# A chain of four cross-attention layers: the value projections of the small attentions as whole 128x128 tiles, placed by head parity on ScalarE

## The reference, cut to what matters

```python
# layer 1
V = (a @ Wv.T).reshape(B, Ta, HEADS, HEAD_DIM).transpose(0, 2, 1, 3)
# layer 2, for ctx (x there) and for x (latents there)
kv = (h @ kv_w + kv_b).reshape(b, p + k_len, NH, DH, 2)
# layer 3, self and cross
qkv = ln_out @ w_qkv + b_qkv
kv = encoder_states @ w_kv + b_kv
...
return jnp.einsum('bhqk,bhkd->bhqd', probs, v)
```

## Time and profile before

| what | before |
|---|---|
| median of 3 runs | 1386.85 us (1385.67 to 1387.0) |
| the profiled execution | 1382.49 us, its span 1380.5 us |
| PE busy | 1287.4 us, 93% |
| PE's weight loads | 975.6 us, 71% |
| VectorE, ScalarE, GpSimd busy | 76%, 59%, 56% |
| L671 (values), records | 1280 in five groups of 256 |
| L882 (placing the values), instructions | 160 |

### The profile page before, as it was taken

One profiled execution on the slowest core, in us unless ns is written; L12 is line 12 of the kernel. 1 busy time (PEld: TensorE's weight loads), 2 busy tenths in 40 slices (PEclk: granted clock), 3 DMA queues, 4 the chain that ended last, 5 costly groups with the idle time before them and its releaser, 6 DMA issues. The chain is left out here.

```text
span 1380.5 us, 34075 instructions
## 1 busy us (share of the span) xinstructions
PE 1287.4 (93%) x12668; PEld 975.6 (71%) x12668; DVE 1049.5 (76%) x2226; ACT 808.0 (59%) x2101; POOL 770.8 (56%) x1056
## 2 busy tenths in 40 slices
PE   6999999999999989999899999999999999979675
PEld 5767668686877868677686867768676776857464
DVE  4788896868789696977968787796969878685642
ACT  4657575565657565565666657565655746554332
POOL 2564575556657474665665557565655656563431
PEclk9999999999999999999999999999999999999896
DMA  8100000000000000000000000000000000000000
GB/s 315 37 3 17 2 19 9 17 11 5 18 6 17 11 17 11 6 17 7 17 7 22 6 10 17 8 17 11 16 11 2 21 7 2 7 1 6 1 4 5
DMA packets 23584, 25.72 MB, mean 19 GB/s; under 512 B 10624, under 2 KB 22912, under 8 KB 23168
## 3 DMA queue, kind: packets, MB, share of 16 engines
q1 hardware_dynamic: 23424, 23.55, 5.4%
HBM read 21.44 MB, written 2.10 MB: 17 GB/s over the span
## 5 line engine op out<-in xcount | busy, mean ns | idle before, releaser
L588 POOL TENSOR_SCALAR p_a<-p_a,rec_a 128x256 f32<-128x256 f32 x512 | 245.8, 497 | 99.1 <-DVE rec_a L543 98.8
L574 ACT ACTIVATE p_a<-bank,nmax_a 128x256 f32<-128x256 f32 x512 | 236.8, 476 | 91.3 <-DVE nmax_a L536 90.7
L536 DVE TENSOR_REDUCE nmax_a<-bank 128x2 f32<-128x512 f32 x256 | 166.9, 680 | 13.5 <-PE bank L486 13.2
L601 PE MATMUL bank<-ident,p_a 128*128 128x128 f32 x1024 | 144.7, 277 | 6.0 <-POOL p_a L588 2.7
L486 PE MATMUL bank<-k_a,q_a 64*128 64x256 f32 x1024 | 138.7, 396 | 2.9 <-ACT p_a L574 1.1
L617 PE MATMUL attended<-p_a,v_a 128*64 128x256 f32 x1024 | 133.9, 389 | 4.2 <-DVE p_a L635 1.6
L601 PEld LDWEIGHTS bank<-ident,p_a 128*128 128x128 f32 x1024 | 113.7, 141 | 33.6 <-issue 25.2
L486 PEld LDWEIGHTS bank<-k_a,q_a 64*128 64x128 f32 x1024 | 91.7, 186 | 32.9 <-issue 22.6
L574 ACT ACTIVATION_READ_ACCUMULATOR p_a<-bank,nmax_a 128x1 f32 x512 | 105.8, 207 | 0.0
L617 PEld LDWEIGHTS attended<-p_a,v_a 128*64 128x64 f32 x1024 | 65.4, 136 | 54.5 <-issue 27.9
L635 DVE COPY p_a<-bank 128x512 f32<-128x512 f32 x128 | 86.1, 679 | 14.7 <-PE bank L601 14.3
(11 more groups left out here) (235 smaller groups left out, 3098.7 us busy)
## 6 DMA issues: line engine op xcount, KB each, us to landing
wb<-in_wb SPq DMA_DIRECT2D x1, 4096.0 KB, 12.6
wc<-in_wc SPq DMA_DIRECT2D x1, 4096.0 KB, 24.3
xc<-in_x SPq DMA_DIRECT2D x16, 128.0 KB, 2.7
xc<-in_ctx SPq DMA_DIRECT2D x16, 128.0 KB, 2.9
c_top<-in_ctx SPq DMA_DIRECT2D x16, 128.0 KB, 2.8
res_a<-in_x SPq DMA_DIRECT2D x16, 128.0 KB, 2.1
k_c<-in_ctx SPq DMA_DIRECT2D x16, 128.0 KB, 2.1
out<-y_out SPq DMA_DIRECT2D x16, 128.0 KB, 1.7
```

Of the source, the lines that this page charges most:

```text
L536: dve.tensor_reduce(nmax_a[:, n, e, :], ps[:, :].rearrange("p (q k) -> p q k", q=KT), AX.X, ALU.max, negate=True).then_inc(A.s["max"], 1)
L574: last = act.activation(p_a[:, j % 2, n, e, qt, :], ps[:, qt * D:(qt + 1) * D], ACT.Exp, bias=nmax_a[:, n, e, qt:qt + 1], accum_out=sum_a[ ...
L588: last = pool.tensor_scalar(p_a[:, j % 2, n, e, qt, :], p_a[:, j % 2, n, e, qt, :], rec_a[:, n, e, qt:qt + 1], 1.0, ALU.mult, ALU.mult)
L601: last = nc.tensor.transpose(ps[:, kt * D + qt * P:kt * D + (qt + 1) * P], p_a[:, j % 2, n, e, qt, kt * P:(kt + 1) * P], ident[:, :])
```

## The change

`pe_values` makes two matmuls instead of eight: all 128 tokens of the pair are the stationary operand, and all 256 columns of the weights are the moving one. The output has the sequence in its row half and the heads in their order. `act_values` makes four copies instead of two, one for each sequence b and parity e, from the bank's row half b to the row half e of `T.v`; where b and e differ, input rows and output rows are different ones. Semaphores and fills are the same in kind and number. The strings of `ORDER` for all five engines, and `BANK`, are written anew: the same letters, each as often as before, in another order. The first letters of SP's and PE's stand here.

```diff
     "sp": (
-        "nssdbenkfdbekfbekfdnkbdnbednkeyfbdnkeyf...
+        "nksskfednbkfedfbebdnkbdnbednkeyfbdnkeyf...
     "pe": (
-        "nnsnnaaaaaaddaadddddaadddsskddkddaaknsddkddnddddkdkakaaadknnkbddakbabakadd...
+        "nknsnnaakaaaaddaadddddaadddsdddnaaddkdsddnkddksdaddaaakdannkbddbabakkkddak...
...
         def pe_values(T, i, name, w, srcT):
             ps = fill_bank(T, nc.tensor, i, name)
-            wv = w.rearrange("p k (g e d) -> p k g e d", e=2, d=HD)
-            for b in range(2):
-                for k in range(KT):
-                    for e in range(2):
-                        last = mm(ps[e * S:(e + 1) * S, b * P:(b + 1) * P], srcT[:, k, b * S:(b + 1) * S], wv[:, k, :, e, :],
-                                  start=k == 0, stop=k == KT - 1)
+            for k in range(KT):
+                last = mm(ps[:, 0:D], srcT[:, k, :], w[:, k, :], start=k == 0, stop=k == KT - 1)
             filled(T, last, i, name)
...
             ps = wait_fill(V, act, i, name)
-            for e in range(2):
-                last = act.activation(T.v[e * S:(e + 1) * S, c, :, :, e, :],
-                                      ps[e * S:(e + 1) * S, 0:D].rearrange("p (b g d) -> p b g d", b=2, d=HD), ACT.Copy)
+            for b in range(2):
+                heads = ps[b * S:(b + 1) * S, 0:D].rearrange("p (g e d) -> p g e d", e=2, d=HD)
+                for e in range(2):
+                    last = act.activation(T.v[e * S:(e + 1) * S, c, b, :, e, :], heads[:, :, e, :], ACT.Copy)
             release(V, last, i, name)
```

More of the change, by code:

```diff
@@ L99 @@
[L99 to L103, removed]
@@ new lines @@
+        "bcbkeakeeeecddeacddcddcddaaaddfnnfabeedadbefddeaaeddedandfdfafdkdnefkkeefdeekkkffbfcfkcckcbdbaadbddcbaaeddeeee"
+        "cddecddcaacdadfafeedbdfaneddebaneddedffnaafekdfeedfdkekeffkkkfbnfkddcdakccbbcabcdbddeaeeeeddedccdaddcaadcdanae"
+        "edbdfbnfddfaeendeddeaadaddffddfneafkeedfdeedfkkfkkkkkbcfcdaccfbbacabdddbdddeaeeeedeccdcannacbdbeedaaefedfdndfa"
+        "deddeddaadffdnfaaefkekefkddeekkkkkbfddcfcccbfbcbabfeaeedeececdcddcddadadanfbfbeefnaeeddeaddendadffdafedkfekefk"
+        "aeekffknbfckccfckkdcdbddbdaabddbcdcedeeeeaecdcddddaadaadfnfbebfdaneeedaeddefdfdafnddekfaneefdkkaekfkbkeffkckbd"
@@ L137 @@
-        "aaaekedeaaffaafaaaeeafkkbbbbfbbeeckckdbbccffdccccaecaecaadadeeeeaecefefeddfffdffffkeeeeffefeeccffkbbkbbkbbfcfc"
-        "ccbcceecceeeeeeecefffeeffeffeffeeccccffcfcccfccfffcfffffffffffffff"),
-    "pool": (
[L140 to L146, removed]
+        "nnknssnknnaaaaaaaaaaadsaadaaaaaddfaanbeasnaaadaaadskanndksadaaaaadanaankkdnakabbaabadbbaabkaandnaadanakaabbaaa"
@@ new lines @@
+        "eaaaefdaaaadnnaffanffffdakeeaaeaandaffefeaaeecacffkfnfbbnccbbdbbkcccdccbbaaceaaeadeeaeeeeaacdfdafeadeaafakkaaf"
+        "fdaaffnfafdnaeaekneaaanadaafafefaenndkffeeccbbbbkffbkcbkcccdcbbcaaeceaadaceeaeeeeaacdfadafeaaaefdaanffnffaffdk"
+        "deaeaaaeaaaaffaafaeaefkkbbbbfbbeecdckkbbccffdccccaecaecdaaadeeaeeecefefeddfffdffffekeeeffefeeccffkbbbkbkbfbccf"
+        "ccbcceecceeeeeeeecfffeeffeffeffeeccccfffccccfccfffcfffffffffffffff"),
+    "pool": (
+        "ssnkaaaaaaaaaaaaaakanakkkaaaakkkaababkaknaaaaeeaaaeekkaeaaeaabbaaaeaeaacecnaaccaaaacceeccaaeffaeaaakffkaakffna"
+        "aeaaffaakaakkkbbcccceecceeccffeaaaeffakkkaffaaaenaaffaakkccbbaakkcceaeccaceecffeaaefafakkfkfaaeaanffaaaacckkbb"
+        "cckaceceakceecaaffeaaeaakfkfakafafaeaanfafacckkkkbbccaacceaeaceecffeaaeaaffakkkfafaaeaaffaacckkkknbbccaacceeee"
+        "accafeafaeaaaakffkkfaafeanafaafaacckkkkbbccaaccceeceeaaefefaaaakffaakkffeanaaaffaaaacckkkkbbcccceecceeffeaaeff"
+        "aakkkffaaeaaffaacakkcankkccbbccccaaeeaeeaffeaaeaffakkkffaaeaaffnaakkaakkccbbcccceecceeaaaaffeaaeaakfkfkaaffnaa"
+        "eaaffaakkccccbbkkcccaeeacaeeaffeaaeaaaffkkkaffeaaaffaccaakknccbbckckceecaeeaaaffeeaaaaffkkkfafaeaaaaffaankkcck"
+        "kbbcccceeceeacaaaffeaeaaffakkkffeaaaaffaaaakkkkbbcceeccccceceaaaaffeekffkkffeffcckkkkbbcccceeeecceeffkefkfffcc"
@@ L167, in fill_places @@
+    "426301452613546124063512346150324615032461503246150324610532461360561302564130254321054321025524653240165324601624"
+    "160260534261452034562103642510642530462153046215340650602165304261530215024653102104160431256041325602650264513062"
+    "140351642035164203516403516403516240351460324605321460532165403216540321654032165043216504215603421560342156034215"
+    "60342156034215603421560342156034125603412")
 def fill_places():
```

87 lines of the change are left out of this document (40 added, 47 removed).

## The result

The changed kernel takes 1378.58 us (median; 1378.4 to 1379.38) against 1386.64 us. The ratio is 0.9944, with a 95% interval of 0.9927 to 0.9961; a second, longer measurement beside another set of runs gave 0.9950 (0.9935 to 0.9964). So the change saves 7 to 8 us, 0.5 to 0.6%. The forecast had the sign right and the size wrong: 17.0 us.

A forecast was written before the change was run, and what follows sets the result against it. It took PE's queue to bound some 1200 of 1380 us: 22.0 - 1.5 - 0.4 - 1.7 - 0.8 - 0.65 = 17.0 us less, so 1386.85 - 17.0 = 1370 us. The range was 1360 to 1381 us.

The forecast's parts named there:

- The price of a change of shape: On PE, each array-shape change between neighbouring steps costs 0.15 to 0.20 us; 133 fewer at 0.165 us save 22.0 us.
- The rival that the price belongs to each change of line or bank: On PE, only the number of steps counts, which stays 1492: 1387 us, no change; chance 0.05.
- part 2: PE's new order: 32 fewer shape changes, 5.3 us; price bounded at 0.14 to 0.20 us each.
- Streaming: In PE's value projections, the streaming itself doesn't shrink: 0.88 us of the old step against 0.87 us after.
- ScalarE: Value copies: four of 269 ns replace two of 376 ns, 26 us more on ScalarE, 0.8 us of it reaching PE.
- The start: On SP, an extra load issued ahead of the raw weights delays PE's first weight product: +0.65 us.
- What of it counts: How much of PE's 22.0 us reaches the run: 1.5, 0.4 and 1.7 us off for last tenth, first tenth and middle.
- The term for growing waits: In PE's middle stretch, a tenth is taken off as waits on other engines become relatively later: -1.7 us.
- the tail: Last tenth of PE's order, a chain over other engines: half of 3.0 us (18 changes) counts, -1.5 us.
- a middle share of PE below 95%: Sign against the forecast: PE's busy share in the middle falling below 95%, where the same 97% was expected.
- waits in the place of work: Rival: over half the saving becomes PE's waits on VectorE, ScalarE and GpSimd softmax chains; 1378 us, chance 0.17.

The follow-up runs named there:

- e3: Kernel before, with each value projection copied by ScalarE in four instructions of 64x128 instead of two of 64x256, none changing rows: ratio 1.0017 to before.
- e4: Changed kernel with the two 64x256 value copies of before put back in place of four of 64x128: ratio 0.9946 to before.
- e1: Changed projection and copies, with the queue orders and banks of the kernel before: ratio 0.9972 to before.
- e5: Changed kernel with one of the two matmuls of each value projection left out: median 1377.26 us, ratio 0.9920 to before.
- e7: Changed kernel with VectorE's row maxima of the big attention taken over half of each row's columns: median 1362.13 us, ratio 0.9817 to before.
- e9: Kernel before with VectorE's row maxima of the big attention taken over half of each row's columns: ratio 0.9900 to before.
- e13: Changed kernel with VectorE's big-attention row maxima over half the columns and GpSimd scaling only half the probability columns: ratio 0.9762 to before.

## Why the prediction was right or wrong

**The price of a change of shape: right.** 0.10 us on leaving and 0.05 to 0.10 on entering carried over to the new steps: L668 at 0.87 us, its neighbours at 1.78 and 1.73 us. Over the run there are 133 changes fewer, 21.9 us by this price; no single row measures that sum, and the page's busy time of PE fell by 16.3 us. The trace agrees here with the Trainium skill's rule that a change of tiling mode drains TensorE ("TensorEngine Tiling (Array Packing)", Key Properties). The rival that the price belongs to each change of line or bank falls: eight records of L662 with the same shape on both sides take 0.89 us (median of 18 rows before), and the next row is always another line or bank. One bound in part 2 is wrong: at the paces that it states, the records from 50 to 1250 us make 1006 us, not 1056. What is left is then 154 us, 0.21 us for each change instead of 0.14, an upper bound and not a lower one, as waits that no row notes lie in it. The price of 0.165 us doesn't rest on it.

**Streaming: right.** 1100.9 and 1099.9 us.

**ScalarE: right in the work, low in its effect.** 271 ns against 269 forecast, 26.2 us more busy (834.2 less 808.0), the copies that change rows like the others (e3, with none that does, has 270 to 271 ns as well). On the time it costs 2.4 us (e3, 1.1 to 3.7) or, taken away again, 0.5 us (e4, within the intervals), where 0.8 was forecast. The Trainium skill's figure ("ScalarE: Activation LUTs", What ACT_TABLE_LOAD costs) of 186 ns + 0.833 ns an element makes 293 ns for these; the trace is 22 ns lower.

**The start: small, as forecast, but not shown.** PE's first weight product starts at 9.13 us instead of 8.79, 0.34 us later and not 0.65. e1, with the loads in the old order, starts it at 9.14 us, so even the 0.34 us may be no more than the scatter of a load's landing.

**The step that failed: "What of it counts".** It says that for some 1200 us "the time is what PE has in its queue, and an edit counts by what it does to PE's pace, and only there in full", and takes off a tenth of what counts in the middle for waits that become later. That sentence rests on PE's 97 to 98% in the windows and on 40 us of noted idle. Both are true and neither makes PE the bound. What is missing is what happens when PE gets faster: e5 shows that from here 34.6 us fewer give 4. The term for growing waits should have been about 10 us instead of 1.7: 22.0 less 1.5, 0.4, 0.65 and ScalarE's 2.4, less the 7 that came. By the two pages PE's idle time grew by 12.2 us, with the shares of ScalarE, the start and the tail in it. The sign that was set for this, a middle share of PE below 95%, didn't show it: the windows have 96.5 and 96.8%, where they had 97.9 and 97.3%. On a stretch of 1200 us one point of that share is already 12 us.

**The rival that won** is the first, waits in the place of work, at 1378 us and with a chance of 0.17. Its own reason, VectorE's 82% and the softmax chains, is half of it: e7 and e9 show VectorE's part, but e13 shows that with VectorE and GpSimd lighter still only 12.5 of 22 us count. The argument against it, "they are 3% of the saturated stretch", reads the size of the present waits as if it were the size that they can reach. That its 1378 us met 1378.58 is in part luck, as its half was a round share that no row gave.

The Trainium skill, "Perfetto Trace Analysis" (Identifying the Most-Contended Engine), finds the engine to work on by occupancy, but for TensorE it rejects the busy share of the matmuls and takes, beside the share of peak arithmetic, that of the weight loads. The prediction leaned on the 93 to 98% of the matmuls. By the skill's shares VectorE (77%) stands ahead of TensorE's weight loads (70%), ScalarE (61%) and GpSimd (56%), and VectorE's line is the one that gave most for each microsecond taken away (0.27). Further down the trace doesn't follow: GpSimd comes next (0.21), ahead of PE (0.1, at most 0.2) and ScalarE (under 0.1), so there the measurement decides against the order by occupancy.

**What stays open**: which waits hold the lost part beyond L685's. The other 5.4 us of the noted growth are spread over many lines at 1.6 us or less each, near what two single traces can tell apart, and what is lost beyond the noted idle time is seen in no row.

## What to carry to other kernels

Where several in-order queues have been fitted to each other, a busy share of 97% says that an engine has little slack, not that taking work off it shortens the run: a saving counts at the rate at which the others let it, here a third of 22 us. Before pricing a saving at one to one, put a dose on the suspected engine in both directions: here +34.6 us cost 17 and -34.6 us gave 4, and that kink showed that PE no longer set the pace alone. And a step is also the cover for a chain beside it: ask what PE reaches sooner, and whether that is ready.

## What the runs showed of the hardware

A change of the array's shape between two steps of fp32 matmuls costs 0.09 us at the step that is left and 0.05 us (transposes, 128*64 tiles) to 0.10 us (128*128 matmuls) at the one that is entered, by the medians of the rows in both traces, and it counts as busy time (133 changes fewer took 16.3 us off PE's).

A copy on ScalarE from rows 0 to 63 of a bank to rows 64 to 127 of a tile, or the other way, costs what one within the same rows does: 253 to 281 ns for all 320 of 64x128 in the changed kernel, and 270 to 271 ns on average in e3, where none crosses. A VectorE maximum over 128x256 in PSUM takes 414 ns against 680 for 128x512, and GpSimd's scaling of 128x128 383 ns against 497 for 128x256, so over half of the latter is not by the element (halving the columns took only 23% off).
